# Second attention's queries and keys packed into two dense blocks of features, on one Trainium2 core

## The reference

```
x = x + jnp.tanh(g_xattn[1]) * _L1_xattn_ref(_layernorm(x, axis=-1), ctx_1024, ctx_1024, ...)

NUM_HEADS = 16; D_K = 16
Q = (query @ Wq + bq).reshape(B, Tq, NUM_HEADS, D_K).transpose(0, 2, 1, 3)
K = (key @ Wk + bk).reshape(B, Tk, NUM_HEADS, D_K).transpose(0, 2, 1, 3)
scores = jnp.einsum('bhtd,bhsd->bhts', Q, K) / jnp.sqrt(jnp.float32(D_K))
attn = jax.nn.softmax(scores, axis=-1)
```

## Time and profile before

| | us |
|---|---|
| median of 3 runs | 1748.5 (1748.27 to 1749.46) |
| the profiled execution, its own time | 1747.4 |
| its span, first to last instruction | 1745.8 |
| PE busy | 1438.3 (82%) |
| DVE busy | 1171.9 (67%) |
| ACT busy | 908.2 (52%) |
| POOL busy | 446.3 (26%) |

### The profile page before, as it was taken

How to read it: one execution, slowest core, us unless ns; L and a number is a source line. 1 busy time by engine, 2 the same in 40 slices (tenths; PEclk the granted TensorE clock), 3 DMA queues, 4 the chain that set the end, 5 groups by cost and what they waited for, 6 DMA issues and landing times.

```text
span 1745.8 us, 36348 instructions
## 1 busy us (share of the span) xinstructions
PE 1438.3 (82%) x12061; PEld 1108.1 (63%) x12062; DVE 1171.9 (67%) x2974; ACT 908.2 (52%) x2701; POOL 446.3 (26%) x608
## 2 busy tenths in 40 slices
PE   2335788898889888898888766199999999999994
PEld 1214465666656565666656533188888888888884
DVE  5657788988998898988998752244444444444442
ACT  1112366676766767676766654144445444455442
POOL 0001012221212212221212110234344344344342
PEclk9556799999999999999999988599999999999997
DMA  6002202231122202222022000653223132142124
GB/s 181 9 0 84 84 20 79 97 97 66 33 97 97 86 31 80 97 97 68 31 88 88 13 7 7 203 184 108 33 30 108 33 105 35 32 105 35 31 30 120
DMA packets 63332, 123.62 MB, mean 71 GB/s; under 512 B 14129, under 2 KB 52139, under 8 KB 59051
## 3 DMA queue, kind: packets, MB, share of 16 engines
q1 hardware_dynamic: 45915, 102.75, 17.2%
q0 software_dynamic: 17312, 19.56, 6.9%
HBM read 78.64 MB, written 48.04 MB: 73 GB/s over the span
## 4 chain that ended last, share of the span: by engine, by line
PE 61%; DVE 23%; ACT 6%; issue 6%; DMA 1%; POOL 1%; SPq 0%; DVEq 0%; ACTq 0%; POOLq 0%
PE bank L1310 16%; PE bank L1312 15%; PE bank L1311 15%; PE bank L1386 5%; PE bank L1399 3%; DVE b_mn L1031 2%; PE bank L1416 2%; PE bank L1422 1%; DVE wm L1113 1%; DVE wm L1109 1%; DVE wm L1101 1%; DVE wm L1115 1%; ACT b_ex L694 1%; PE bank L1602 1%; ACT a_z L669 1%
## 5 line engine op out<-in xcount | busy, mean ns | idle before, releaser
L1310 PE MATMUL bank<-split_room,wm 128*128 128x256 f16 x1152 | 315.0, 273 | 8.3 <-issue 6.8
L1287 DVE SCALAR_TENSOR_TENSOR split_room<-bank,b12e,split_room 128x256 f32<-128x256 f32 x288 | 138.1, 484 | 265.0 <-ACT split_room L817 264.9
L1311 PE MATMUL bank<-split_room,wm 128*128 128x256 f16 x1152 | 314.9, 273 | 0.0
L1312 PE MATMUL bank<-split_room,wm 128*128 128x256 f16 x1152 | 314.8, 273 | 0.0
L694 ACT ACTIVATE b_ex<-bank,b_mn 128x120 f32<-128x120 f32 x512 | 177.4, 359 | 138.8 <-DVE b_mn L1031 129.5
L817 ACT ACTIVATE split_room<-bank,b12e 128x256 f32<-128x256 f32 x288 | 134.1, 470 | 195.5 <-PE bank L1312 193.7
L1311 PE MATMUL bank<-wm,split_room 128*128 128x256 f16 x576 | 157.0, 273 | 0.0
L1312 PE MATMUL bank<-wm,split_room 128*128 128x256 f16 x576 | 157.0, 273 | 0.0
L1310 PE MATMUL bank<-wm,split_room 128*128 128x256 f16 x576 | 157.0, 273 | 0.0
L1386 PE MATMUL bank<-b_k,b_q 128*128 128x480 f32 x256 | 130.2, 590 | 26.3 <-ACT b_q L766 26.3
L640 POOL DMA_INDIRECT acc<-split_room,m_cur x72 | 115.5, 1604 | 133.3 <-ACT split_room L831 106.9
(11 more groups left out here) (358 smaller groups left out, 3754.4 us busy)
## 6 DMA issues: line engine op xcount, KB each, us to landing
split_room<-in_L_ffn_W SPq DMA_DIRECT2D x48, 512.0 KB, 8.1
wsplit<-split_room SPq DMA_DIRECT2D x16, 1536.0 KB, 6.4
wm<-wsplit SPq DMA_DIRECT2D x16, 1536.0 KB, 8.7
acc<-x SPq DMA_DIRECT2D x17, 256.0 KB, 7.0
xin<-in_x SPq DMA_DIRECT2D x16, 256.0 KB
rows<-r_row SPq DMA_DIRECT2D x16, 256.0 KB, 2.1
ct<-in_ctx SPq DMA_DIRECT2D x16, 120.0 KB
cb<-in_ctx SPq DMA_DIRECT2D x16, 120.0 KB, 2.2
```

What stands on the lines that cost most here:

```text
L1287: dve.scalar_tensor_tensor(m_h[:, c % 3], bank[c % 4][:, TILE:2 * TILE], b12e[:, p, 1, c:c + 1], m_s[:, c % 2], ALU.add, ALU.mult).then_in ...
L1310: pe.matmul(o, lh, rh, start=start, stop=False)
L1311: pe.matmul(o, ll, rh, start=False, stop=False)
L1312: return pe.matmul(o, lh, rl, start=False, stop=stop)
```

## The change

Queries and keys keep their natural order of features, which makes two dense blocks of 128 instead of four padded ones. PE makes them with 2 x 7 = 14 and 2 x 6 = 12 matmuls. A block of 128 rows now holds eight heads, two in each group of 32 rows, and `b_k` has two copies of each block: in one the rows of the even heads are kept, in the other those of the odd. The selection is made as ACT copies the keys, by a scale per partition that is 0 or 1 (two new columns of constants, `C_M`). That takes 8 instructions of 32 by 240 where 4 of 32 by 480 stood; ACT's `B.q` takes 2 of 128 by 256 where 4 stood. The score matmuls stay as many and as large, and so does all that follows them. `prep_b` loses two memsets and works on dense weights, 9 small transfers at the start go, and one memset of `bqk`.

The orders of all engines are rewritten. They are turned, so that a step begins at another point of the cycle: PE's begins at `B.t3`, DVE's at `A.s0`, and `prep_f` and `prep_b` come later by the entries that now stand ahead of the step's border. They are changed in places, too: DVE's `R.rank` goes behind `B.s1`, `B.s3` goes ahead of `F.p1`; PE's `F.ht0` goes behind `B.t1` and `F.ht1` behind `B.t3`, `B.s4` and `B.p2`; `R.logit` goes ahead of `A.t` on PE and behind `B.q` on ACT; POOL's `R.scatter` goes ahead of `W0`, and `W2` behind `F.ln`; SP's `B.load` for the same sample comes a step later.

```diff
-        b_q = sb("b_q", [P, QUAD, T])
-        b_k = sb("b_k", [P, QUAD, QUAD, S])
+        b_q = sb("b_q", [P, NK, T])
+        b_k = sb("b_k", [P, NK, 2, QUAD, S])
...
+    c[:, C_M:C_M + 2] = np.arange(P)[:, None] // K1 % 2 == np.arange(2)
...
-            "SP": ("A.load/-1 W/0 B.out/3 R.rank/3 B.load/0").split(),
-            "POOL": ("B.ln/2 R.ln/3 A.ln/-1 W0/0 W1/0 W2/0 F.ln/0 R.scatter/3").split(),
-            "ACT": ("B.t1/3 F.ht0/2 B.t2/3 B.s3/3 A.s0/0 F.ht1/2 B.t3/3 B.s4/3 B.s5/3 B.t4/3 B.s6/3 B.r3/3 F.z/1 A.s1/0 "
-                "A.t0/0 B.t5/3 B.o0/3 A.t1/0 B.s7/3 B.t6/3 F.t/1 B.t7/3 B.r7/3 B.o1/3 A.ot/0 F.gu0/1 B.z/2 F.gu1/1 R.z/3 "
-                "B.ct/2 B.zt/2 R.t/3 A.z/-1 F.gu2/1 A.t/-1 F.gu3/1 R.logit/3 B.k/2 B.q/2 B.s0/2 B.s1/2 B.t0/2 B.s2/2").split(),
-            "DVE": ("B.v/3 A.rk/0 B.s1/3 F.q1b/2 A.r0/0 B.s2/3 F.q1c/2 A.r1/0 F.p1/2 B.s3/3 F.ht0/2 A.s0/0 W0/1 B.s4/3 "
-                "F.ht1/2 B.s5/3 F.ln/1 B.s6/3 B.rx0/3 W1/1 A.s1/0 B.p3/3 F.q/1 B.o0/3 B.s7/3 F.p/1 F.d1/2 A.p0/0 A.p1/0 "
-                "B.rx1/3 F.t/1 W2/1 B.p7/3 B.ln/2 B.o1/3 A.ot/0 B.out/3 F.gu0/1 R.ln/3 A.out/0 A.ln/-1 F.gu1/1 F.q0a/1 "
-                "B.ct/2 B.zt/2 F.gu2/1 R.t/3 R.logit/3 A.t/-1 F.gu3/1 F.q0b/1 F.q1a/1 F.q0c/1 R.rank/3 B.s0/2 F.p0/1").split(),
-            "PE": ("B.t0/3 B.s2/3 B.p0/3 A.q1/0 B.t1/3 B.t2/3 B.s3/3 B.p1/3 A.s0/0 F.ht1/2 B.t3/3 B.s4/3 B.p2/3 B.s5/3 "
-                "A.s1/0 B.t4/3 B.s6/3 A.t0/0 B.p3/3 F.d0/2 B.p4/3 B.t5/3 B.s7/3 A.t1/0 A.p0/0 F.d1/2 B.t6/3 A.p1/0 F.t/1 "
-                "B.p5/3 B.t7/3 B.p6/3 A.ot/0 B.p7/3 F.gu0/1 B.out/3 A.out/0 F.gu1/1 B.ct/2 B.zt/2 R.t/3 F.gu2/1 A.t/-1 "
-                "R.logit/3 F.gu3/1 B.k/2 B.q/2 R.rank/3 B.s0/2 B.v/2 A.kv/-1 B.s1/2 A.q0/-1 F.ht0/1").split(),
+            "SP": ("A.load/-1 B.load/1 W/0 B.out/3 R.rank/3").split(),
+            "POOL": ("A.ln/-1 R.scatter/3 W0/0 W1/0 F.ln/0 W2/0 B.ln/1 R.ln/2").split(),
+            "ACT": ("B.t0/3 B.s2/3 B.t1/3 F.ht0/2 B.t2/3 B.s3/3 B.t3/3 A.s0/0 F.ht1/2 B.s4/3 B.s5/3 B.t4/3 B.s6/3 B.r3/3 "
+                "F.z/1 A.s1/0 A.t0/0 B.t5/3 B.o0/3 A.t1/0 B.s7/3 B.t6/3 F.t/1 B.t7/3 B.r7/3 B.o1/3 A.ot/0 F.gu0/1 B.z/2 "
+                "F.gu1/1 R.z/3 B.ct/2 B.zt/2 R.t/3 A.z/-1 F.gu2/1 A.t/-1 F.gu3/1 B.k/2 B.q/2 R.logit/3 B.s0/2 B.s1/2").split(),
+            "DVE": ("A.s0/0 B.s4/3 W0/1 B.s5/3 F.ht1/2 F.ln/1 B.s6/3 B.rx0/3 W1/1 A.s1/0 B.p3/3 F.q/1 B.o0/3 B.s7/3 F.p/1 "
+                "F.d1/2 B.rx1/3 A.p0/0 A.p1/0 F.t/1 W2/1 B.p7/3 B.ln/2 B.o1/3 A.ot/0 B.out/3 F.gu0/1 R.ln/3 A.out/0 "
+                "A.ln/-1 F.gu1/1 B.ct/2 B.zt/2 F.q0a/1 F.gu2/1 R.t/3 R.logit/3 A.t/-1 F.gu3/1 F.q0b/1 F.q1a/1 F.q0c/1 "
+                "B.s0/2 F.p0/1 B.v/2 B.s1/2 R.rank/3 A.rk/-1 B.s2/2 F.q1b/1 A.r0/-1 F.q1c/1 A.r1/-1 B.s3/2 F.p1/1 F.ht0/1").split(),
+            "PE": ("B.t3/3 B.s4/3 B.p2/3 F.ht1/2 B.s5/3 A.s1/0 A.t0/0 B.t4/3 B.s6/3 B.p3/3 F.d0/2 B.p4/3 B.t5/3 B.s7/3 "
+                "F.d1/2 A.t1/0 A.p0/0 B.t6/3 A.p1/0 F.t/1 B.p5/3 B.t7/3 B.p6/3 A.ot/0 B.p7/3 F.gu0/1 B.out/3 A.out/0 "
+                "F.gu1/1 B.ct/2 B.zt/2 R.t/3 F.gu2/1 R.logit/3 A.t/-1 F.gu3/1 B.k/2 B.q/2 R.rank/3 B.s0/2 A.kv/-1 B.v/2 "
+                "B.s1/2 A.q0/-1 B.t0/2 B.s2/2 A.q1/-1 B.p0/2 B.t1/2 F.ht0/1 B.t2/2 B.s3/2 B.p1/2 A.s0/-1").split(),
...
-                    last = act.activation(b_k[h, :, j], bank[4][h, 0:QUAD * S].rearrange("p (c s) -> p c s", c=QUAD), ACT.Copy)
+                    for a in range(2):
+                        last = act.activation(b_k[h, :, a, j], bank[4][h, 0:NK * S].rearrange("p (c s) -> p c s", c=NK), ACT.Copy, scale=C[h, C_M + a:C_M + a + 1])
...
-                for c in range(QUAD):
-                    src = bank[3 - c // 2][:, (c % 2) * T:(c % 2 + 1) * T]
-                    last = act.activation(b_q[:, c], src, ACT.Identity, bias=bqk[:, c:c + 1])
+                for c in range(NK):
+                    last = act.activation(b_q[:, c], bank[3][:, c * T:(c + 1) * T], ACT.Identity, bias=bqk[:, c:c + 1])
...
-                for w in (wq1, wk1):
-                    link(dve.memset(w[:, :, :, :, :].bitcast(f32), 0.0))
...
-                for c in range(QUAD):
-                    pe.matmul(bank[4][:, c * S:(c + 1) * S], bk_h[:, c * P:(c + 1) * P], ones_h[:, 0:S], start=True, stop=False)
+                for c in range(NK):
+                    f = slice(c * P, (c + 1) * P)
+                    pe.matmul(bank[4][:, c * S:(c + 1) * S], bk_h[:, f], ones_h[:, 0:S], start=True, stop=False)
```

More of the change, by code:

```diff
@@ L43 @@
 C_G = 1032
-C_N = C_G + 48
+C_M = C_G + 48
+C_N = C_M + 2
 def shape_constants():
@@ L932, in prep_b @@
                 for i, w in enumerate((wq1, wk1)):
-                    for k in range(NK):
-                        hi, lo = (w[:, j, k].rearrange("p (a n) d -> p a n d", a=2)[:, :, :, 0:K1] for j in range(2))
-                        split(st1[:, i, k].rearrange("p (n a d) -> p a n d", a=2, d=K1), hi, lo)
+                    split(st1[:, i], w[:, 0], w[:, 1])
                 split(st1[:, 2], wv1[:, 0], wv1[:, 1])
@@ L1383, in stage @@
                                       start=True, stop=False)
-                        for c in range(h0 // side, (h0 + QUAD) // side):
-                            at = (c * side - h0) * S
-                            last = pe.matmul(sbk[:, at:at + side * S], q[:, c, t * P:(t + 1) * P], kk[:, c] if G is B else kk[:, :, :],
-                                             start=G is B, stop=G is B or at > 0)
+                        if G is A:
+                            for c in range(h0 // side, (h0 + QUAD) // side):
+                                at = (c * side - h0) * S
+                                last = pe.matmul(sbk[:, at:at + side * S], q[:, c, t * P:(t + 1) * P], kk[:, :, :], start=False, stop=at > 0)
+                        else:
+                            r = k % per
+                            last = pe.matmul(sbk[:, 0:QUAD * S], q[:, r % 2, t * P:(t + 1) * P], kk[:, r % 2, r // 2], start=True, stop=True)
                         last.then_inc(G.s_mm, 1)
@@ L1512, in b_k_ @@
                 pe.wait_ge(B.ct_lo, b + 1)
-                for c in range(QUAD):
-                    pe.matmul(bank[4][:, c * S:(c + 1) * S], bk_h[:, c * P:(c + 1) * P], ones_h[:, 0:S], start=True, stop=False)
+                for c in range(NK):
+                    f = slice(c * P, (c + 1) * P)
+                    pe.matmul(bank[4][:, c * S:(c + 1) * S], bk_h[:, f], ones_h[:, 0:S], start=True, stop=False)
                     for k in range(NK):
-                        wh, wl = (wk1[:, i, k, 4 * c:4 * c + 4].rearrange("p h d -> p (h d)") for i in range(2))
-                        last = three(bank[4][:, c * S:(c + 1) * S], wh, b_ct[:, 0, k], wl, b_ct[:, 1, k], False, k == NK - 1)
+                        last = three(bank[4][:, c * S:(c + 1) * S], wk1[:, 0, k, f], b_ct[:, 0, k], wk1[:, 1, k, f], b_ct[:, 1, k], False, k == NK - 1)
                 last.then_inc(B.k_mm, 1)
@@ L1521, in b_q_ @@
                 pe.wait_ge(B.zt_lo, b + 1)
-                for c in range(QUAD):
-                    o = bank[3 - c // 2][:, (c % 2) * T:(c % 2 + 1) * T]
+                for c in range(NK):
+                    f = slice(c * P, (c + 1) * P)
                     for k in range(NK):
-                        wh, wl = (wq1[:, i, k, 4 * c:4 * c + 4].rearrange("p h d -> p (h d)") for i in range(2))
-                        last = three(o, wh, b_zt[:, 0, k], wl, b_zt[:, 1, k], k == 0, k == NK - 1)
+                        last = three(bank[3][:, c * T:(c + 1) * T], wq1[:, 0, k, f], b_zt[:, 0, k], wq1[:, 1, k, f], b_zt[:, 1, k], k == 0, k == NK - 1)
                 last.then_inc(B.q_mm, 1)
```

28 lines of the change are left out of this document (11 added, 17 removed).

## The result

The changed kernel takes 1798.19 us (median of 4 runs, 1795.69 to 1800.48) against 1748.38 (4 runs, 1746.82 to 1749.46). The ratio is 1.028, interval 1.026 to 1.030: slower by 50 us, well outside the range of the prediction (1725 to 1756). The profiled execution took 1798.3 with a span of 1796.2.

A forecast was written before the change was run, and what follows sets the result against it. PE and DVE, both at 90% in the steady part, were taken as nearly tied. Steady +5.2, first steps -6.7, last steps -3 and first full samples -1.5 gave -6.0 us: 1741.4 profiled, 1742.5 median, range 1725 to 1756.

The forecast's parts named there:

- the one on POOL: POOL's W0 and W1 leave DVE's L1183 and meet other DVE work: nothing booked, bounds 0.15 us either way.
- The prediction's account of that chain: Steady part: PE without pause from 688.59 to before 715.25, ACT to 719.6, PE to 727.9, then ACT's B.q.
- PE's and ACT's parts: B.k and B.q matmuls halved on PE; on ACT eight key copies take 3.3 us, queries 0.84 for 1.57.
- When the scores start: B.s0's scores on PE start 1.35 us sooner; PE idle 3.1 us ahead of them, DVE waits 0.6.
- The steady gain: Steady part with every engine at its speed: reciprocals sooner, 0.5 us a period gained, bounds 0 and 1.4.
- The clock: PE's wait behind B.q lowers its clock in 9 of 13 samples, each losing 0.8 us against before.
- rival 2: PE's clock stays down longer or falls again in the next waits: 1755.5 us, lower end 1747.7; chance 0.2.
- First steps: Start of the run: less DVE work in prep_b, and waits covered by prep_b and prep_f: -6.7 us, bounds -4 and -9.
- The first full samples: Early full samples, not yet bound by DVE, give 1 to 2 us; taken as -1.5.
- Last steps: Last samples, with PE's clock low: keys and queries copied sooner; -3 us, bounds 0 and -6.

The follow-up runs named there:

- e14: e13 with POOL's new order (scatter ahead of the weight splits) put back: 1770.2 us, ratio 1.0129 to the kernel before.
- e13: e12 with its two fillers around A.s0 made of products over 128 rows, from the fifth sample on: 1740.0 us, ratio 0.9940 to before.
- e1: The changed kernel with only POOL's order of before restored (weight splits ahead of the scatter): 1760.5 us, ratio 1.0062 to before.
- e12: e1 plus three fillers of unread PE products: behind B.q, and one-row ones ahead of and behind A.s0's scores: 1747.4 us, ratio 0.9999 to before.
- e2: The kernel before with POOL's new order alone: 1775.4 us, ratio 1.0153 to before.
- e4: The kernel before, with its padded blocks, given all the new orders: 1814.0 us, ratio 1.0371 to before.
- e3: The changed kernel's dense blocks with all orders of before: 1748.6 us, ratio 0.9994 to before.

## Why the prediction was wrong

**The step that failed** is the one on POOL: "they meet DVE's work elsewhere, so I book nothing, bounds 0.15 either way". The term put at nothing, 2 us over 13 samples by its bounds, measured +30 us by itself (e14 against e13), 37.7 with the clock that it took down (after against e1). I had the mechanism's trace in front of me, L1183 at 834 ns in the median where 681 is possible, and took the relief as its whole size. That place was cheap because, of what DVE does during POOL's splits there, only L1183 is large and works in SBUF alone. Before, in the timelines of POOL and DVE:

```profile
719.00 3.50 POOL L567 TENSOR_SCALAR split_room<-split_room 128x1024 f16<-128x1024 f32 x3 [0.74 <-DMA split_room<-in_L_ffn_W]
...
720.78 0.82 DVE L1183 TENSOR_TENSOR r_row<-r_z,r_row 128x512 f16<-128x512 f32 x1
```

I did not lay the three splits, some 1.04 us each, over the new neighbours: two of them, one behind the other, on an addition of 0.42 us for which `A.s0` waits. The bound should have been their 2.07 us times 13, 27 us. The chain of before, which the earlier trace rows shows in parts, has both rotary additions of a sample on it; the second is the one that POOL came to hold:

```profile
681.68 0.43 DVE a_t L1021
...
684.74 0.43 DVE a_t L1021
```

The prediction's account of that chain starts behind them, at 688.59 (and its "PE without a pause" from there passes over a wait of 0.45 us for the reciprocals at 695.83).

**PE's and ACT's parts** were right. `B.k` and `B.q` are halved (`B.q` takes 1.31 us, from 693.71 to 695.02), the eight copies take 3.23 us for the 3.3 forecast, the queries 0.84.

**When the scores start:** the wait of PE ahead of `B.s0` came to 2.85 us with the new orders (forecast 3.1), DVE waited 0.80 for the scores (forecast 0.6).

**The steady gain** of 0.5 us a period with the clock up was right in sign and near in size: 56.03 to 55.68 in e13, 0.35. But it needed POOL's old order and three fillers, and what of it the new places on PE give was not tested.

**The clock:** the mechanism was right, both sizes were too small. I took 9 of 13 samples and 0.8 us above the period of before. With POOL back (e1) the period of 57.11 stands against 55.68 with the clock held (e13), 1.4 us in the mean over all periods, and the whole run loses 20.5 us. What I missed is the second place of falls, around `A.s0`, where e12 shows them without a wait close ahead, as well as the price: forecast +5.2 us for the steady part, clock included, measured 57.11 - 56.03 = 1.1 a period, 14 us, in e1, POOL's hold apart. That is rival 2, and by e1 alone (1760.5) it would have been the case, at a higher price than its 1755.5: even with POOL's order kept, the time would have lain above the range.

**First steps:** -6.7 forecast, -6.2 measured at sample 0's queries, copied from 217.40; the keys' copy began at 214.1, forecast 214. Only the sum was compared, not its parts. The first full samples were to give 1.5 more; in e13 the first period is 54.35 us for 55.70 before.

**Last steps:** -3 forecast. The last three samples gain 1.1 us in e13, and behind the last queries e13 loses 5.6 us (694.8 against 689.2), so the ends together are 4.5 worse. Behind the last queries e2 and e4, without dense blocks, lose 2.5 and 2.3, e3 6.5. I have no experiment on it; this stays open.

The sum for the changed kernel, in runs: 1798.2 = 1748.4 - 8.4 (e13 against before: what the change gives with nothing in its way) + 30.2 (POOL's hold, e14) + 28.0 (the clock, after against e14). The comparisons were made on several chips, whose runs of before had medians from 1748.0 to 1750.6, so each term is good to some 3 us; by the ratios, each to the runs of before beside it, the three are -10.5, +33 and +26.

## What to carry to other kernels

An instruction moved on one engine is priced at the place where it lands: lay its duration over what the other engines do there, and look first for VectorE operations with both operands in SBUF while GpSimd reads SBUF. Work saved on an engine that then waits longer can cost its clock, and that price is read from the stretches behind the wait, not from the wait. When one stage looks ready for fewer copies or matmuls, put the order's other moves in one at a time; here two entries of one queue outweighed everything else in the change.

## What the hardware showed that was not expected

- POOL's two splits, in 2.06 and 2.07 us, held a VectorE addition of 0.42 us for 1.95 and 2.52 us in all, while a multiplication of the same shape with one operand in a bank ran beside them in 0.41.
- TensorE's granted clock fell to 1.2 GHz in stretches without idle time. In e12, from 627 to 630 us, PE is busy all of each window:

```profile
627.00:628.00 1.00, 1.00 (x5) 0.73 (x5) 1.00 (x4) 0.28 (x1) 0.00 (x0) 0.62 0.00 0
628.00:629.00 1.00, 1.00 (x2) 0.00 (x0) 0.39 (x1) 0.81 (x3) 0.00 (x0) 0.50 0.00 0
629.00:630.00 1.00, 1.00 (x11) 0.49 (x11) 0.76 (x2) 0.63 (x3) 0.00 (x0) 0.50 0.00 0
```

  One-row products in the place of the waits left 21 low windows, products over 128 rows of about the same length none. The two differ in type and count as well, and the second begin with the fifth sample, so which property matters is not shown. The Trainium skill (TensorE: Matmul & The Clock Gate, the table of the two states) tells the states apart as idle and busy; in these windows PE is busy throughout by its rows, and the granted clock is 0.62 and 0.50.
- The four unmasked copies of the keys (32x480) take 2.26 us, the eight masked ones (32x240) 3.21 to 3.23: two half copies cost 0.24 us more than a whole one.
